# Two wide attention layers in one phase, with keys and values of the second layer's first two pairs projected before its normalised rows

## The chip, the cores and the metric

The kernel runs on one core of a Trainium2 chip. The metric is the device time of one execution in microseconds; less is better. The five engines are TensorE (PE in the rows; PEld is its weight load), VectorE (DVE), ScalarE (ACT), GpSimd (POOL) and SyncE (SP, which here only issues DMAs). Each runs its own program in order and waits for the others on semaphores.

## What is computed

A chain of four cross-attention modules on x, two batches of 256 rows and 256 features, against one context of 512 rows per batch. The first module has 16 narrow heads and an MLP. The second, in which the change lies, has two wide layers, 16 heads of 128 features each, and then an MLP. The third and fourth have 16 narrow heads each. One wide layer is, cut from the reference:

```python
def _cross_attention(q_in, kv_in, wq, bq, wk, bk, wv, bv, wo, bo, bias_k, bias_v):
    qh = (q_in @ wq + bq).reshape(b, q_len, H, K)
    kh = (kv_in @ wk + bk).reshape(b, t, H, K)
    vh = (kv_in @ wv + bv).reshape(b, t, H, K)
    kh = concatenate([kh, bias_k], axis=1); vh = concatenate([vh, bias_v], axis=1)
    weights = softmax(einsum('bqhk,bthk->bhqt', qh, kh) / sqrt(K))
    ctx = einsum('bhqt,bthk->bqhk', weights, vh).reshape(b, q_len, H * K)
    return ctx @ wo + bo

x = x + _cross_attention(_layer_norm(x, ln1_scale, ln1_offset), xf_1, ...)
x = x + _cross_attention(_layer_norm(x, ln2_scale, ln2_offset), xf_2, ...)
```

Both layers attend to the same context (xf_1 and xf_2 are the same tensor), with weights of their own. Only the queries depend on x. Everything is float32; products run as three matmuls on a high and a low part of each operand (`product3`, lines 82 to 84).

## The kernel before

`program` runs one `Phase` after another. A phase holds its buffers and semaphores, and at its end (line 140) it clears the semaphores and lets all engines meet at a barrier (its waits appear in rows as L141). `wide_attention` is one phase, run twice, for i = 1 and 2.

A wide layer works on 8 pairs of heads (`PAIRS`). For a pair there are ten projections of the pair's weights: two for queries, ("q", 0) and ("q", 1), four for keys and four for values (`PROJ`). Each is a job: PE fills one of four PSUM banks (`Ring`), ACT writes the high part from it to SBUF, and DVE writes the low part and frees the bank (lines 1189 or 1191, and 1238 or 1240). q, k, v, w, wo and stage are double-buffered by the pair's parity. The weights of pair p come by one DMA of SP into `stage`, and POOL scales and splits them: L1032, L1035 and L1036 for w, L1043 and L1044 for wo. For pair 0, ACT and DVE split the first three chunks (L1195, L1246), since POOL would be late.

A pair has four units (`UN`), one for each head and batch; g counts units. In the loop of unit g PE issues: scores of g, transposes of the probabilities of g - 1, projections for the next pair (`SHARES[u]`: 3, 3, 2 and 2), the output product of g - 2 into `sums`, and the product with V of g - 1. DVE takes the maximum (L1279), writes the low parts of the transposed probabilities, computes the inverse sums (L1290 to L1292), normalises the probabilities (L1294), and writes the low parts of projections and of the attended values. ACT takes the exponentials (L1215). The last pair of a layer has no next pair, so its units have no projections.

At the head of a layer, SP issues the first chunk of weights (the keys'), then four small loads (norm scales L703, `cols` L1012, `bk` L1013, `out_bias` L1014), then the other three chunks (L1008) and the weights of pair 1 (L1020). DVE computes row statistics of x (L111, L115, L123), POOL the root (`NormParts.root`, L711), DVE the normalised rows (L725), the two other weight splits, `bias_product` and the scaled `cols` (L1254, L1255), and adds the output bias to x, four operations (L1260). Only then it writes the low parts of the first four keys. PE projects four keys, then transposes the normalised rows (L740), which need the banks of the first keys, then four values, two queries and the small bias scores (L1129, L1131), and waits until DVE has their negative (L1270) before the first scores. POOL splits pair 1's weights right after pair 0's wo; for pair 2 it waits until the queries of pair 0 have been projected.

At the end of a layer, PE transposes the collected bias probabilities (L1160) after the last output product, ACT copies them (L1226), PE adds their product with the bias values (L1164), and DVE adds `sums` to x (L1304).

## Time and profile before

| | us |
|---|---|
| median of the timed runs | 1140.93 |
| lowest and highest of 3 | 1139.7, 1142.56 |
| span of the profiled execution | 1145.1 |
| its time with what lies around the span | not recorded; the span alone stands 4.2 above the median |
| first wide layer (head to the last bias product), in the profile | about 229 to 521 |
| second wide layer | about 521 to 815 |

The busy shares of the span are 84% for PE, 72% for DVE, 53% for ACT and 29% for POOL. They average stages with different limits: the two wide layers take half of the span, and what the change is worth must be read from the stretch around their border. A row of the timeline gives the start in us from the start of the span, the duration, engine, line, operation, what is written <- what is read with shapes, how many such instructions are merged, and in brackets how long the engine sat idle before and which engine ended that. Names carry no layer number: both layers' buffers are called L1a.

### The profile page before, as it was taken

What the parts mean: (1) busy time and instruction counts of PE and PEld (TensorE: products, weight loads), DVE (VectorE), ACT (ScalarE), POOL (GpSimd) and SP (SyncE); (2) the same over time, 40 slices, a digit from 0 to 9 for tenths busy, and PEclk for the clock granted to TensorE, in tenths of its full rate; (3) what the DMA queues carried; (4) which work ended last, traced back from release to release, by engine and by line L of the source; (5) the groups of instructions that cost most, each with busy time, mean ns of one, the idle gap of its engine ahead of it and who ended that gap; (6) DMA issues with size and microseconds to landing.
All of it is one profiled execution on the core that took longest, in us unless ns stands there. A gap on an engine that the chain in (4) does not pass through costs nothing. (4 is left out here: it accounts for less than half of the span.)

```text
span 1145.1 us, 17853 instructions
## 1 busy us (share of the span) xinstructions
PE 956.2 (84%) x6548; PEld 806.1 (70%) x6548; DVE 823.1 (72%) x1627; ACT 606.0 (53%) x1371; POOL 331.5 (29%) x324
## 2 busy tenths in 40 slices
PE   4788886569999999975999999998586798478958
PEld 3666665557888888963898899887475466465647
DVE  3377757976787887776678878777674587747865
ACT  2488873034555555642455556554424587257842
POOL 4245541441112222004102222200005355525520
PEclk8889998878999999997999999999798699789989
DMA  5985106140001110003101111000304920195120
GB/s 176 234 143 61 16 1 253 46 153 1 21 18 38 38 38 1 1 1 117 38 1 37 38 37 38 1 1 1 116 1 111 177 43 1 51 187 73 21 79 19
DMA packets 38242, 69.49 MB, mean 61 GB/s; under 512 B 7462, under 2 KB 23336, under 8 KB 35596
## 3 DMA queue, kind: packets, MB, share of 16 engines
q1 hardware_dynamic: 38156, 68.35, 24.6%
q8 instruction: 53, 0.87, 0.3%
q14 instruction: 33, 0.27, 0.1%
HBM read 57.31 MB, written 11.02 MB: 60 GB/s over the span
## 5 line engine op out<-in xcount | busy, mean ns | idle before, releaser
L1189 ACT CAST L1a_probsT_hi<-L1a_bank 128x512 fp32r<-128x512 f32 x128 | 68.8, 589 | 92.6 <-PE L1a_bank L1085 92.6
L1043 POOL TENSOR_SCALAR L1a_wo_hi<-L1a_stage 128x512 fp32r<-128x512 f32 x16 | 11.3, 707 | 347.8 <-PE L1a_sums L84 336.8
L1279 DVE TENSOR_REDUCE L1a_top<-L1a_scores 128x2 f32<-128x1024 f32 x64 | 78.2, 1222 | 35.2 <-PE L1a_scores L84 35.2
L1215 ACT ACTIVATE L1a_probs<-L1a_scores,L1a_neg_max 128x512 f32<-128x512 f32 x128 | 86.8, 684 | 30.3 <-DVE L1a_bias_shifted L1283 24.7
L82 PE MATMUL L1a_bank<-L1a_probsT_hi,L1a_v_hi 128*128 128x256 f32 x256 | 72.5, 283 | 11.7 <-DVE L1a_probsT_lo L1238 11.0
L1238 DVE TENSOR_TENSOR L1a_probsT_lo<-L1a_bank,L1a_probsT_hi 128x512 fp32r<-128x512 f32 x128 | 81.9, 681 | 0.1
L1191 ACT ACTIVATE L1a_attended_hi<-L1a_bank,L1a_cols 128x256 fp32r<-128x256 f32 x64 | 30.3, 474 | 91.5 <-PE L1a_bank L84 91.5
L82 PE MATMUL L1a_bank<-L1a_w_hi,ctxT_hi 128*128 128x256 f32 x256 | 75.7, 296 | 0.0
L83 PE MATMUL L1a_bank<-L1a_w_lo,ctxT_hi 128*128 128x256 f32 x256 | 73.1, 286 | 0.0
L84 PE MATMUL L1a_bank<-L1a_w_hi,ctxT_lo 128*128 128x256 f32 x256 | 73.0, 285 | 0.0
L400 POOL TENSOR_SCALAR L0a_probs<-L0a_probs,L0a_inverse 128x768 f32<-128x768 f32 x64 | 57.2, 906 | 53.2 <-DVE L0a_inverse L651 53.2
L637 DVE TENSOR_REDUCE L0a_neg_max<-L0a_scores 128x1 f32<-128x768 f32 x64 | 58.6, 954 | 18.1 <-PE L0a_scores L487 16.0
L84 PE MATMUL L1a_bank<-L1a_probsT_hi,L1a_v_lo 128*128 128x256 f32 x256 | 71.4, 279 | 0.0
L83 PE MATMUL L1a_bank<-L1a_probsT_lo,L1a_v_hi 128*128 128x256 f32 x256 | 71.4, 279 | 0.0
L1085 PE MATMUL L1a_bank<-ident,L1a_probs 128*128 128x128 f32 x512 | 66.2, 272 | 0.0
L82 PE MATMUL L1a_bank<-ctxT_hi,L1a_w_hi 128*128 128x512 f32 x128 | 53.5, 418 | 14.8 <-DVE L1a_w_lo L1246 14.8
L1085 PEld LDWEIGHTS L1a_bank<-ident,L1a_probs 128*128 128x128 f32 x512 | 59.6, 140 | 8.3
L576 ACT ACTIVATE L0a_probs<-L0a_scores,L0a_neg_max 128x768 f32<-128x768 f32 x64 | 57.5, 909 | 11.0 <-DVE L0a_neg_max L637 11.0
L82 PE MATMUL L1a_scores<-L1a_k_hi,L1a_q_hi 128*128 128x512 f32 x128 | 53.3, 416 | 10.8 <-DVE L1a_v_lo L1238 5.5
L1240 DVE SCALAR_TENSOR_TENSOR L1a_attended_lo<-L1a_bank,L1a_cols,L1a_attended_hi 128x256 fp32r<-128x256 f32 x64 | 30.9, 482 | 39.9 <-ACT L1a_attended_hi L1191 39.4
L82 PEld LDWEIGHTS L1a_bank<-L1a_probsT_hi,L1a_v_hi 128*128 128x128 f32 x256 | 48.2, 188 | 13.5 <-DVE L1a_probsT_lo L1238 12.4
L1294 DVE TENSOR_SCALAR L1a_probs<-L1a_probs,L1a_inverse 128x512 f32<-128x512 f32 x128 | 56.1, 480 | 0.0
(407 smaller groups left out, 3157.9 us busy)
## 6 DMA issues: line engine op xcount, KB each, us to landing
L1a_stage<-in_L_w SPq DMA_DIRECT2D x14, 1024.0 KB, 4.8
L0m_fold_wq<-in_L_wq SPq DMA_DIRECT2D x2, 2048.0 KB, 20.4
L0a_k_stack<-L0a_k_dram SPq DMA_DIRECT2D x12, 192.0 KB
L0a_w_qkv<-L0a_k_dram SPq DMA_DIRECT2D x12, 192.0 KB
L0a_probs<-in_L_wo SPq DMA_DIRECT2D x1, 2048.0 KB, 10.0
L0a_probsT<-in_L_wo SPq DMA_DIRECT2D x1, 2048.0 KB, 11.2
L0m_stage<-in_L_wm SPq DMA_DIRECT2D x4, 512.0 KB, 6.0
L0m_fold_bias_k<-in_L_bias_k SPq DMA_DIRECT2D x2, 1024.0 KB, 16.0
```

Source lines behind the costliest of these rows:

```text
L82: nc.tensor.matmul(out, lh, rh, start=start, stop=False, skip_group_check=loose)
L83: nc.tensor.matmul(out, lh, rl, start=False, stop=False, skip_group_check=loose)
L84: return nc.tensor.matmul(out, ll, rh, start=False, stop=stop, skip_group_check=loose)
L400: nc.gpsimd.tensor_scalar(probs[:, slot, :], probs[:, slot, :], inverse[:, small:small + 1], 1.0, ALU.mult, ALU.mult).then_inc(normed, 1)
L576: nc.scalar.activation(probs[:, m % probs_slots, :], slot_scores(m), ACT.Exp, bias=neg_max[:, small:small + 1], accum_out=row_sum[:, small ...
L637: nc.vector.tensor_reduce(neg_max[:, small:small + 1], slot_scores(m), AX.X, ALU.max, negate=True).then_inc(max_done, 1)
L1085: last = nc.tensor.transpose(ring.bank(job)[:, kt * P:(kt + 1) * P], probs[:, g % 2, qt, kt * P:(kt + 1) * P], keep["ident"][:, :])
L1189: nc.scalar.copy(out, source).then_inc(ring.hi_done, 1)
L1215: nc.scalar.activation(probs[:, g % 2, qt, :], scores[:, qt, :], ACT.Exp, bias=neg_max[:, g % 2, qt:qt + 1], accum_out=row_sum[:, g % 2, q ...
L1238: nc.vector.tensor_tensor(out[1], source, raw(out[0]), ALU.subtract).then_inc(ring.freed_by(job), 1)
L1279: link(nc.vector.tensor_reduce(top[:, :], scores[:, :, :], AX.X, ALU.max))
L1294: nc.vector.tensor_scalar(probs[:, s, qt, :], probs[:, s, qt, :], inverse[:, qt:qt + 1], None, ALU.mult).then_inc(normed, 1)
```

## The change

`wide_attentions` is one phase for both layers: `LAYERS` = 2, pairs 0 to 15 (`ALL`), units 0 to 63, one set of buffers. Small tensors exist once per layer (`cols`, `bk`, `out_bias`, `bias_product`, the norm's `scale_shift`); all of them are loaded at the head of layer 1, eight small loads instead of four, and both `bias_product` and `cols` are computed there. The buffers of the norm are shared.

- Units of pair 7 (the last of layer 1) project the keys and values of pair 8 (layer 2's first), two in each unit.
- After layer 1's last products PE projects the keys of pair 9, transposes layer 2's normalised rows, projects the values of pair 9, and then the queries of pair 8 and the bias scores (`queries`).
- Units of pair 8 project only the two queries of pair 9, in the first two units.
- POOL runs on through all 16 pairs; the root of layer 2's norm stands after the split of w and before the split of wo for pair 9.
- Between the layers DVE waits for `sums_full`, adds the sums to x and signals `sums_free`, for which the first output product of layer 2 waits.
- The transposes of the bias probabilities stand ahead of the last product with V, and ACT's copy ahead of its high part.

```diff
+    LAYERS = 2
+    ALL = LAYERS * PAIRS
     UN = 2 * B
+    GL = PAIRS * UN
     SK = S // P
     scale = float(DW) ** -0.5
-    PROJ = [("q", 0), ("q", 1), ("k", 0, 0), ("k", 0, 1), ("k", 1, 0), ("k", 1, 1)] + [("v", t) for t in range(0, CT, 2)]
-    SHARES = [PROJ[0:3], PROJ[3:6], PROJ[6:8], PROJ[8:10]]
-    FIRST = PROJ[2:]
+    QS = [("q", 0), ("q", 1)]
+    KV = [("k", 0, 0), ("k", 0, 1), ("k", 1, 0), ("k", 1, 1)] + [("v", t) for t in range(0, CT, 2)]
+    PROJ = QS + KV
+
+    def share(p, u):
+
+        if p == PAIRS:
+            return KV[2 * u:2 * u + 2]
+        if p == PAIRS + 1:
+            return QS[u:u + 1]
+        return (PROJ[0:3], PROJ[3:6], PROJ[6:8], PROJ[8:10])[u] if p < ALL else []
...
+        START = KV[:4] + ["norm0", "norm1"] + KV[4:] + QS + ["bias_scores"]
+        AGAIN = KV[:4] + ["norm0", "norm1"] + KV[4:] + QS + ["bias_scores"]
+        job_of, n = {}, 0
+        for item in START:
+            job_of[(0, item) if item in PROJ else (item, 0)] = n
+            n += 1
+        for layer in range(LAYERS):
+            if layer:
+                for item in AGAIN:
+
+                    job_of[(PAIRS + (item in KV), item) if item in PROJ else (item, layer)] = n
+                    n += 1
+            for gl in range(GL + 1):
+                g = layer * GL + gl
+                p, u = divmod(g, UN)
+                if gl:
+                    for qt in range(2):
+                        job_of["T", g - 1, qt] = n
+                        n += 1
+                if gl < GL:
+                    for item in share(p + 1, u):
+                        job_of[p + 1, item] = n
+                        n += 1
+                if gl == GL:
+                    job_of["bias", layer] = n
+                    n += 1
+                if gl:
+                    job_of["V", g - 1] = n
...
+                    for i in range(LAYERS):
+                        parts[i].load(sp, io)
+                        sp.dma_start(cols[i][:, :, :], io[f"L1_cols{i + 1}"]).then_inc(small_loaded, 16)
+                        sp.dma_start(bk[i][:, :], io[f"L1_bk{i + 1}"]).then_inc(small_loaded, 16)
+                        sp.dma_start(out_bias[i][:, :], io[f"L1_bo{i + 1}"].partition_broadcast(P)).then_inc(small_loaded, 16)
+            for p in range(1, ALL):
                 if p == 2:
                     sp.wait_ge(first_lo, 3)
                 if p >= 2:
                     sp.wait_ge(wo_ready, p - 1)
-                sp.dma_start(stage[p % 2][:, :], io[f"L1_w{i}"][p]).then_inc(loaded[p % 2], 16)
+                sp.dma_start(stage[p % 2][:, :], io[f"L1_w{p // PAIRS + 1}"][p % PAIRS]).then_inc(loaded[p % 2], 16)
...
+                if p == PAIRS + 1:
+                    parts[1].root(nc, pool)
                 if p >= 2:
                     pool.wait_ge(out_done, UN * (p - 1))
...
+                if g % GL == 0 and g:
+                    pe.wait_ge(sums_free, g // GL)
...
+            for layer in range(LAYERS):
+                if layer:
+                    pe.wait_ge(w_ready, PAIRS + 1)
+                for n, item in enumerate(KV):
+                    if n in (0, 4) and layer == 0:
+                        pe.wait_ge(first_lo, 1 if n == 0 else 2)
+                    project(PAIRS + 1 if layer else 0, item)
+                    if n == 3:
+                        parts[layer].transpose(nc, pe, ring, keep)
+                queries(layer)
+                for gl in range(GL + 1):
+                    g = layer * GL + gl
+                    p, u = divmod(g, UN)
+                    if gl < GL:
+                        if u == 0:
+                            for item in PROJ:
+                                ring.wait_evacuated(pe, job_of[p, item])
+                            if gl == 0:
+                                ring.wait_evacuated(pe, job_of["bias_scores", layer])
+                        score(g)
+                    if gl:
+                        transposes(g - 1)
+                    if gl < GL and p + 1 < ALL:
+                        if u == 0:
+                            pe.wait_ge(w_ready, p + 1)
+                        for item in share(p + 1, u):
+                            project(p + 1, item)
+                    if gl >= 2:
+                        output(g - 2)
+                    if gl == GL:
+                        bias_probabilities(layer)
+                    if gl:
+                        product_v(g - 1)
+                output(layer * GL + GL - 1)
+                bias_products(layer)
...
+                        job = job_of["bias", layer]
+                        act.wait_ge(ring.full, job + 1)
+                        nc.scalar.copy(bias_probsT[:, :], ring.bank(job)[:, :]).then_inc(ring.freed_by(job), 1)
+                    if gl:
+                        j, hh, b, h = unit(g - 1)
+                        high(job_of["V", g - 1], attended[(g - 1) % 2][0][:, :], cols[layer][:, 2, h:h + 1], Q)
...
+            for layer in range(LAYERS):
+                p0 = layer * PAIRS
+                if layer:
+                    dve.wait_ge(sums_full, layer)
+                    for t in range(RT):
+                        last = nc.vector.tensor_tensor(keep["x"][:, t, :], sums[:, t, :], keep["x"][:, t, :], ALU.add)
+                    last.then_inc(sums_free, 1)
+                    dve.wait_ge(sums_free, layer)
+                parts[layer].normalise(nc, dve, link, keep["x"], 1e-5, True)
+                if layer == 0:
+                    for n, c in enumerate(FIRST_ORDER[:3]):
+                        low_weights(n + 1, c)
+                    dve.wait_ge(small_loaded, 48 * LAYERS)
+                    for i in range(LAYERS):
+                        link(nc.vector.tensor_tensor(bias_product[i][:, :], cols[i][:, 0, :], cols[i][:, 1, :], ALU.mult))
+                        nc.vector.tensor_scalar(cols[i][:, 0, :], cols[i][:, 0, :], scale, None, ALU.mult).then_inc(cols_scaled, 1)
+                    dve.wait_ge(cols_scaled, LAYERS)
+                    dve.wait_ge(ones_set, 2)
+                dve.wait_ge(parts[layer].normed_ready, 1)
+                for t in range(RT):
+                    last = nc.vector.tensor_tensor(keep["x"][:, t, :], keep["x"][:, t, :], out_bias[layer][:, :], ALU.add)
+                last.then_inc(bias_ready, 1)
+                for n, item in enumerate(KV):
+                    p = p0 + 1 if layer else 0
+                    low(job_of[p, item], destination(p, item), bias_of(p, item))
+                    if n == 3:
+                        split_norm(layer)
```

## Rows read from the trace of the kernel before

**Rows 1.** Busy time by stretch: us, each engine's busy us (instructions), clock, DMA.
```profile
489.00:516.00 27.00, 20.71 (x150) 18.43 (x148) 19.32 (x46) 13.47 (x35) 0.00 (x0) 1.00 0.00 1
...
558.00:564.00 6.00, 5.73 (x18) 4.58 (x19) 1.76 (x4) 1.39 (x5) 0.16 (x1) 0.72 0.00 0
```

**Rows 2.** TensorE in order of time, at the border of the two wide layers.
```profile
519.12 1.99 PE L1164 MATMUL L1a_sums<-bias_values,L1a_bias_probsT 128*128 128x256 f32 x8 [0.68 <-ACT L1a_bias_probsT L1226]
528.76 0.79 PE L82 MATMUL L1a_bank<-ctxT_hi,L1a_w_hi 128*128 128x512 f32 x1 [7.66 <-DVE L1a_w_lo L1246]
...
542.10 1.94 PE L740 MATMUL L1a_bank<-ident,L1a_normed 128*128 128x128 f32 x8 [4.76 <-DVE L1a_k_lo L1240]
...
558.27 0.50 PE L82 MATMUL L1a_scores<-L1a_k_hi,L1a_q_hi 128*128 128x512 f32 x1 [2.65 <-DVE neg_bias_scores L1270]
```

**Rows 3.** VectorE in order of time, the same border.
```profile
521.15 1.42 DVE L1304 TENSOR_TENSOR x_rows<-L1a_sums,x_rows 128x256 f32<-128x256 f32 x4 [4.24 <-PE L1a_sums L1164]
523.49 1.41 DVE L111 BATCH_NORM_STATS2 L1a_stats<-x_rows 128x6 f32<-128x256 f32 x4 [0.93 <-PEq L141]
...
526.73 1.38 DVE L725 TENSOR_SCALAR L1a_normed<-x_rows,L1a_moments,L1a_rstd 128x256 f32<-128x256 f32 x4 [1.21 <-POOL L1a_rstd L711]
...
533.97 7.31 DVE L1260 TENSOR_TENSOR x_rows<-x_rows,L1a_out_bias 128x256 f32<-128x256 f32 x4
541.21 2.71 DVE L1240 SCALAR_TENSOR_TENSOR L1a_k_lo<-L1a_bank,L1a_bk,L1a_k_hi 128x512 fp32r<-128x512 f32 x4
```

**Rows 4.** GpSimd in order of time, the same border.
```profile
525.67 1.02 POOL L711 TENSOR_TENSOR L1a_rstd<-L1a_shifted,L1a_power 128x4 f32<-128x4 f32 x1 [1.50 <-DVE L1a_shifted L123]
...
537.54 3.47 POOL L1036 TENSOR_TENSOR L1a_w_lo<-L1a_stage,L1a_w_hi 128x1536 fp32r<-128x1536 f32 x1
540.98 0.79 POOL L1043 TENSOR_SCALAR L1a_wo_hi<-L1a_stage 128x512 fp32r<-128x512 f32 x1
...
543.20 0.62 POOL L1032 TENSOR_SCALAR L1a_stage<-L1a_stage 128x512 f32<-128x512 f32 x1
```

**Rows 5.** VectorE, normalised rows of the narrow layer L3a.
```profile
985.38 6.82 DVE L725 TENSOR_SCALAR L3a_normed<-x_rows,L3a_moments,L3a_rstd 128x256 f32<-128x256 f32 x4 [1.22 <-POOL L3a_rstd L711]
```

**Rows 6.** TensorE in order of time, units without projections and the layer's end.
```profile
499.70 0.39 PE L82 MATMUL L1a_scores<-L1a_k_hi,L1a_q_hi 128*128 128x512 f32 x1
...
504.20 0.36 PE L82 MATMUL L1a_bank<-L1a_probsT_hi,L1a_v_hi 128*128 128x256 f32 x1 [1.37 <-DVE L1a_probsT_lo L1238]
...
505.64 0.39 PE L82 MATMUL L1a_scores<-L1a_k_hi,L1a_q_hi 128*128 128x512 f32 x1
...
517.84 0.60 PE L1160 MATMUL L1a_bank<-ident,L1a_bias_probs 128*128 128x128 f32 x4
```

**Rows 7.** TensorE in order of time: starts of scores in units with projections.
```profile
455.86 0.50 PE L82 MATMUL L1a_scores<-L1a_k_hi,L1a_q_hi 128*128 128x512 f32 x1 [0.55 <-DVE L1a_v_lo L1238]
...
472.99 0.40 PE L82 MATMUL L1a_scores<-L1a_k_hi,L1a_q_hi 128*128 128x512 f32 x1
...
480.25 0.40 PE L82 MATMUL L1a_scores<-L1a_k_hi,L1a_q_hi 128*128 128x512 f32 x1
...
587.88 0.50 PE L82 MATMUL L1a_scores<-L1a_k_hi,L1a_q_hi 128*128 128x512 f32 x1
```

**Rows 8.** ScalarE in order of time, second exponential of layer 2's first unit.
```profile
563.29 0.68 ACT L1215 ACTIVATE L1a_probs<-L1a_scores,L1a_neg_max 128x512 f32<-128x512 f32 x1
```

**Rows 9.** VectorE in order of time, low parts of two queries.
```profile
565.46 1.40 DVE L1240 SCALAR_TENSOR_TENSOR L1a_q_lo<-L1a_bank,L1a_cols,L1a_q_hi 128x512 fp32r<-128x512 f32 x2
```

**Rows 10.** SyncE's issues in order of time, head of layer 1.
```profile
231.18 0.43 SPq L1014 DMA_DIRECT2D L1a_out_bias<-in_L_bo  x1
231.66 1.38 SPq L1008 DMA_DIRECT2D L1a_stage<-in_L_w  x3
```

**Rows 11.** ScalarE in order of time, head of layer 1: weight splits.
```profile
236.37 1.29 ACT L1195 ACTIVATE L1a_w_hi<-L1a_stage 128x512 fp32r<-128x512 f32 x2 [3.78 <-DMA L1a_stage<-in_L_w]
```

**Rows 12.** VectorE in order of time, head of layer 1: output bias onto x.
```profile
239.13 7.32 DVE L1260 TENSOR_TENSOR x_rows<-x_rows,L1a_out_bias 128x256 f32<-128x256 f32 x4
```

323 lines of the change are left out of this document (139 added, 184 removed).

## The prediction

> **What bounds the kernel now.** I read first the busy times by stretch, then TensorE (PE) in order of time across the border between the two wide layers, then VectorE (DVE), GpSimd (POOL) and ScalarE (ACT) over the same stretch, each time looking for what ended the last wait. Inside a wide layer PE is the bound: a unit of attention (one head, one batch) with two projections takes 7.26 us, 472.99 to 480.25, and PE has no gap in it [rows 7]. It stops being the bound where projections are missing. In a layer's last pair of heads there is nothing to project, and a unit takes 5.94 us [rows 6], with 1.37 us of idle PE in front of each product with V, ended by DVE's low part of the transposed probabilities. PE is busy 20.71 of 27 us there, at a granted clock of 1.00 [rows 1].
>
> The border is worse. PE ends the last bias product at 519.12 + 1.99 = 521.11. It starts the next keys at 528.76, because DVE has just split freshly loaded weights; it ends them at 542.10 - 4.76 = 537.34 and waits until 542.10 for a key's low part from DVE; it starts the first scores at 558.27 [rows 2]. From the last product to the transposes of the normalised rows pass 20.99 us. DVE's share of that: adding sums to x (from 521.15), 0.93 us of phase change, statistics, normalising (from 526.73), two weight splits, then four additions of the output bias that take 7.31 us together, and the keys' low parts from 541.21 [rows 3]. Those additions are long because POOL splits the weights of pair 1 beside them: its 3.47 us operation ends at 541.01, and the fourth addition ends at 541.28 [rows 3, 4]. Each of the four gets through in a gap between two POOL operations.
>
> **The change, part by part.** T is the end of layer 1's bias product, 521.11 before. I count pairs through both layers (0 to 7, 8 to 15) and units likewise (28 to 31 are pair 7, 32 to 35 pair 8).
>
> *The border (A).* One phase goes, with its barrier, its first weight load and the split of these weights on ACT and DVE: pair 9's keys and values are projected first, from weights that POOL split during pair 7. So PE starts keys at T and needs no more than the 8.6 us it took before at a mostly low clock, 528.76 to 537.34 [rows 2]. What is late next is DVE, in program order: sums into x until T + 1.46 (1.42 us, as at 521.15); statistics as before, which took from 523.49 to POOL's start at 525.67, 2.2 us, so POOL starts the root at T + 3.75 and ends it at T + 4.8 (1.02 us) [rows 3, 4]. Then come four normalising operations, 1.38 us undisturbed [rows 3]. They are not undisturbed now. POOL stands directly behind the root with wo of pair 9 and the scaling of pair 10's weights, three operations that took 540.98 to 543.82, 2.84 us [rows 4]. No row has this DVE line beside those POOL lines. Below: 1.38 us, ends at T + 6.2. Above: the same line in a later stage, beside POOL's memsets, took 6.82 us [rows 5], ends at T + 11.6. I take the middle way that the four bias additions show, one DVE operation for each gap of POOL: two or three wait, and the last ends some 0.35 us after POOL, at T + 8.1. The bias additions then find POOL waiting for the queries of pair 8, and cost about 1.4 us (as at 521.15, the same size) instead of 7.31: T + 9.5. The first low part of a key (4 in 2.71 us) frees the bank at T + 10.3, and the transposes start. PE's keys are done by T + 8.6 at the worst, so they stay hidden. Gain: 20.99 - 10.3 = 10.7 us. From the transposes to the first scores the order is unchanged, values, queries, bias scores, 16.17 us [rows 2]. The idle of PE ahead of the transposes stays about 4.7 us, so I keep the cold start of what follows.
>
> *Pair 7 gets eight projections (B).* Two in each unit, so its units become those of 7.26 us instead of 5.94 [rows 6, 7]: 4 x 1.32 = 5.3 us. POOL now also splits weights for pairs 8 and 9 during pairs 6 and 7, as in the middle of a layer. There it costs one DVE delay per pair, seen as 0.55 us of idle PE ahead of a unit's scores [rows 7]: 2 x 0.5. Cost 6.3 us. If more projections or waits hid in these units, the full pair's measured length already has them.
>
> *Pair 8 loses eight of ten (C).* Before: 558.27 to 587.88, 29.6 us [rows 2, 7]. After: unit 32 has one projection, and the next scores start when both exponentials are through: 563.29 + 0.68 = 563.97 [rows 8], so 5.8 us. Unit 33 is a thin unit of 5.94 with one query's low part, 1.40 / 2 = 0.7 us [rows 9], ahead of DVE's maximum: 6.6. Units 34 and 35 have none: 5.94 each. Sum 24.3, gain 5.3 us. So B and C are nearly a plain move: the hole in PE's work goes from pair 7 to pair 8.
>
> *Bias tail (D).* The transposes of the bias probabilities now stand before the product with V, which gives ACT time for the copy. Between 517.84 and 519.12 pass 1.28 us [rows 2, 6]; about 0.25 of it moves into the product's start, 1.0 us is saved, in both layers: 2.0 us.
>
> *Layer 1's head (E).* SP issues eight small loads instead of four between the first and second weight chunk. One costs 0.48 us of queue (231.18 to 231.66) [rows 10]: 1.9 us later for the values', queries' and wo chunks, and for the load of pair 1's weights behind them. Waiting on them are ACT, whose split of the second chunk started at 236.37 when its load landed [rows 11], and POOL; behind both stand DVE's bias additions (from 239.13) [rows 12] and the transposes. The small loads also take room on the DMA engines: 0 to 1 us more, I take 0.3. DVE has two more short operations ahead of the additions, which cost one gap of POOL, the 0.79 us operation of the kind at 540.98 [rows 4]: 0.7. Sum 2.9 us. Bounds: 0 (if the landing is hidden by other waits) and 5.7 (1.9, 1 us of traffic, and all three POOL operations of the 2.84 us above in the way).
>
> Sum: -10.7 + 6.3 - 5.3 - 2.0 + 2.9 = -8.8 us. The span of 1145.1 becomes 1136.3. The profiled execution is 4.2 us longer than the median of the timed runs; an absolute difference carries over, so the time is 1140.9 - 8.8 = 1132.1.
>
> **The rivals.**
> 1. *The border gives more.* The normalising operations pass before POOL starts (T + 6.2 instead of T + 8.1), the wait of PE shrinks to under 3 us, and the clock does not fall. For: DVE and POOL both start within 0.1 us of the root's end, 526.73 against 525.67 + 1.02 [rows 3, 4]. Against: 6.82 us in the other stage [rows 5]. Price 1.9 plus some 1.3 of warm transposes and values: 1128.9.
> 2. *The head costs its upper bound* and DVE and POOL meet once more in pairs 7 and 8 (1 us): 1132.1 + 2.8 + 1 = 1135.9. For: DMA rows say nothing of eight in a row.
> 3. *The clock stays low through pair 8 (slower).* The scores before unit 32 start after 2.65 us of waiting, and the clock granted from 558 to 564 is 0.72 of full speed, so part of it ran at 1.2 GHz and part at 2.4 [rows 1]. Before, ten projections in a dense row followed; now units with gaps. At 1.2 GHz the about 19 us of PE work of pair 8 (24.3 less four gaps of 0.9 to 1.4) take 38: + 14.3, so 1146.4. It decides from about 12 us of extra work time on, that is if nearly the whole pair runs low. Against it: units with the same gaps in pair 7 ran at 1.00 [rows 1, 6], though they entered warm. The Trainium skill (TensorE: Matmul & The Clock Gate, section on the second HAM failure mode, psum-queue depth-cycling) tells of a kernel whose short idle times between groups of matmuls made the clock swing between its levels; by it pair 8 would lie between 24.3 and 38 us, where my sum has 24.3, and the trace of thin units disagrees.
> 4. *The work ahead is not ahead.* If POOL split pair 9's weights only after T, PE would start its keys some 6 us late (0.62 of scaling, 3.47 for the low half and, I estimate, half of that for the high half [rows 4]), and the wait for DVE would hide all but about 2 to 4 us: 1135. Against: POOL is idle for most of a pair, and the stage buffer is free from pair 7's start.
>
> **How the numbers follow.** Forecast 0.58, with its own range 1129.5 to 1134.5; rival 1 0.18; rival 2 0.12; rival 4 0.04; rival 3 0.05; 0.03 for a slip of some microseconds that ends within no change. About 0.3%, or 3.4 us, is what a measurement of this kernel can tell from no change. Faster by more than that (under 1137.5): the first four and a part of their spread, 0.89; same 0.06; slower 0.05. The range 1126 to 1137 takes in the forecast and rivals 1, 2 and 4, with the spread of the timed runs (1139.7 to 1142.6) around them.
>
> **What would show it.** In the profile after: PE's keys follow the last bias product without a gap; transposes of normalised rows about 10.3 us after it; four normalising operations of 2.5 to 3.5 us together, beside POOL's wo, and four bias additions of about 1.4 us; pair 7 about 29.6 us and pair 8 about 24.3 us from scores to scores; a granted clock of 1.00 from some 8 us after the start of pair 8; bias products right behind the last output product; in layer 1's head the second chunk landing about 2 us later and the transposes about 3 us later. A clock of 0.5 in pair 8, bias additions still near 7 us in layer 2, or keys waiting for POOL's weights would make the prediction wrong.

## The result

| | us | ratio to the kernel before, 95% interval |
|---|---|---|
| before, 10 runs beside it | 1141.47 (1137.25 to 1147.08) | |
| changed kernel, 10 runs | 1135.98 (1129.81 to 1140.35) | 0.9945 [0.9921, 0.997] |
| changed kernel, once more, 7 runs | 1136.63 (1131.45 to 1141.13) | 0.993 [0.9905, 0.9956] |

The change makes the kernel faster, by 6.3 us in the first comparison (0.9945 of 1141.47; interval 3.4 to 9.0) and 8.0 us in the second (0.993 of 1144.24, the median of 24 runs of the kernel before beside it). The forecast was 8.8 us less, 1132.1, with 1126 to 1137 as range. The profiled span went from 1145.1 to 1131.1 us, 14 us less; that is more than the timed runs give, and the experiments will show why one pair of profiles can't be taken for the difference.

The page of the changed kernel, busy time of each engine and share of the span:

```profile
span 1131.1 us, 17854 instructions
PE 956.8 (85%) x6548; PEld 809.0 (72%) x6548; DVE 817.2 (72%) x1624; ACT 603.5 (53%) x1367; POOL 336.1 (30%) x325
```

Its busy times by stretch (duration, then busy us and instructions of PE, PEld, DVE, ACT, POOL, the granted clock, DMA share, GB/s); they answer [rows 1]. The first line is pair 7, which was thin (without projections) and is now filled; then come the stretch from the transposes of the normalised rows to layer 2's first scores, the first unit of pair 8, and the rest of pair 8:

```profile
493.00:522.00 29.00, 27.52 (x199) 25.50 (x198) 21.42 (x44) 14.99 (x35) 7.62 (x6) 1.00 0.10 37
533.00:550.00 17.00, 14.16 (x92) 13.60 (x93) 10.55 (x14) 5.51 (x9) 4.89 (x2) 0.80 0.05 19
550.00:557.00 7.00, 5.92 (x16) 4.40 (x17) 2.24 (x7) 2.12 (x6) 0.00 (x0) 0.68 0.00 0
557.00:576.00 19.00, 15.27 (x101) 13.25 (x100) 15.25 (x37) 9.85 (x25) 0.00 (x0) 1.00 0.01 1
```

PE has no hole left between the projections and products of pair 7 (27.5 of 29 us busy, where it was 20.7 of 27; the 1.5 us that are missing stand at its end, ahead of two output products). Pair 8 is the thin one now (15.3 of 19 us), and it runs at a granted clock of 1.00 from 557 on, though its first unit ran at a mean of 0.68.

TensorE of the changed kernel in order of time, at the border and through pair 8; it answers [rows 2, 6]:

```profile
521.04 1.89 PE L1149 MATMUL L1a_sums<-bias_values,L1a_bias_probsT 128*128 128x256 f32 x8
522.58 0.58 PE L72 MATMUL L1a_bank<-ctxT_hi,L1a_w_hi 128*128 128x512 f32 x1
...
533.00 1.94 PE L731 MATMUL L1a_bank<-ident,L1a_normed 128*128 128x128 f32 x8 [4.61 <-DVE L1a_k_lo L1287]
...
550.01 0.77 PE L72 MATMUL L1a_scores<-L1a_k_hi,L1a_q_hi 128*128 128x512 f32 x1 [2.85 <-DVE neg_bias_scores L1337]
...
556.17 0.50 PE L72 MATMUL L1a_scores<-L1a_k_hi,L1a_q_hi 128*128 128x512 f32 x1 [1.07 <-ACT L1a_probs L1262]
...
567.09 0.35 PE L72 MATMUL L1a_bank<-L1a_probsT_hi,L1a_v_hi 128*128 128x256 f32 x1 [1.37 <-DVE L1a_probsT_lo L1285]
...
574.60 0.40 PE L72 MATMUL L1a_scores<-L1a_k_hi,L1a_q_hi 128*128 128x512 f32 x1
```

The last bias product has no wait before it any more, and the keys of pair 9 start right behind it, with no idle time in brackets. The product ends at 521.04 + 1.89 = 522.93, the transposes of the normalised rows start at 533.00: 10.07 us, where it was 20.99. Pair 8 goes from 550.01 to 574.60, 24.6 us.

VectorE and then GpSimd over the same border, answering [rows 3] and [rows 4]:

```profile
522.97 1.42 DVE L1310 TENSOR_TENSOR x_rows<-L1a_sums,x_rows 128x256 f32<-128x256 f32 x4 [2.85 <-PE L1a_sums L1149]
524.42 1.41 DVE L101 BATCH_NORM_STATS2 L1a_stats<-x_rows 128x6 f32<-128x256 f32 x4
...
527.65 3.08 DVE L716 TENSOR_SCALAR L1a_normed<-x_rows,L1a_moments,L1a_rstd 128x256 f32<-128x256 f32 x4 [1.21 <-POOL L1a_rstd L702]
530.76 1.43 DVE L1325 TENSOR_TENSOR x_rows<-x_rows,L1a_out_bias 128x256 f32<-128x256 f32 x4
532.11 2.72 DVE L1287 SCALAR_TENSOR_TENSOR L1a_k_lo<-L1a_bank,L1a_bk,L1a_k_hi 128x512 fp32r<-128x512 f32 x4
```

```profile
506.83 0.11 POOL L699 MEMSET L1a_power<- 128x4 f32 x1
526.59 1.03 POOL L702 TENSOR_TENSOR L1a_rstd<-L1a_shifted,L1a_power 128x4 f32<-128x4 f32 x1 [19.64 <-DVE L1a_shifted L113]
527.60 0.62 POOL L1069 TENSOR_SCALAR L1a_wo_hi<-L1a_stage 128x512 fp32r<-128x512 f32 x1
528.30 1.26 POOL L1070 TENSOR_TENSOR L1a_wo_lo<-L1a_stage,L1a_wo_hi 128x512 fp32r<-128x512 f32 x1
529.65 0.62 POOL L1056 TENSOR_SCALAR L1a_stage<-L1a_stage 128x512 f32<-128x512 f32 x1
```

The phase change between sums and statistics is gone. POOL had w of pair 9 split by 506.83, 16 us ahead. The normalising operations take 3.08 us instead of 1.38, through POOL's three operations, and the four additions of the output bias take 1.43 us instead of 7.31.

All the profiles, cut at the same events, in us. "Head" is from the first weight load of layer 1 to its first scores; "border" from the end of layer 1's bias product to the transposes; "to scores" from there to layer 2's first scores; "pair 7" ends with the bias product; a steady pair is the median of pairs 1 to 5 and 9 to 13, scores to scores; "wide" is both layers together, from the first weight load to the first load of the MLP behind them. The kernels below changed are the experiments of the next section.

| kernel | head | border | to scores | pair 7 | pair 8 | steady pair | wide |
|---|---|---|---|---|---|---|---|
| before | 34.61 | 20.99 | 16.17 | 33.44 | 29.61 | 32.36 | 587.89 |
| before_again | 31.82 | 19.54 | 16.70 | 33.45 | 30.31 | 32.36 | 585.47 |
| changed | 32.83 | 10.07 | 17.01 | 37.14 | 24.59 | 32.51 | 576.16 |
| after_again | 36.70 | 10.07 | 17.11 | 37.17 | 24.61 | 32.51 | 580.05 |
| merged_only | 37.48 | 10.08 | 16.50 | 35.86 | 30.02 | 32.51 | 585.10 |
| spread | 32.95 | 10.07 | 14.16 | 37.13 | 25.60 | 32.52 | 574.21 |
| wo_later | 32.49 | 8.38 | 16.39 | 37.14 | 24.58 | 32.51 | 573.59 |
| neg_on_act | 30.44 | 10.08 | 14.77 | 37.15 | 24.62 | 32.52 | 569.77 |
| few_waits | 32.95 | 10.08 | 16.55 | 37.14 | 24.60 | 32.58 | 576.18 |
| wait_order | 36.04 | 10.07 | 17.56 | 37.17 | 24.57 | 32.33 | 577.49 |
| small_loads_later | 31.25 | 10.06 | 17.22 | 37.13 | 24.58 | 32.49 | 574.89 |
| head_pool_later | 29.14 | 10.06 | 17.00 | 37.14 | 24.57 | 32.52 | 572.02 |
| combined | 29.27 | 8.38 | 11.18 | 37.17 | 25.11 | 32.58 | 566.32 |
| combined_order | 29.11 | 8.36 | 11.60 | 37.17 | 25.63 | 32.33 | 563.87 |

Read the columns downwards. Border, pair 7, pair 8 and the steady pair are the same to a tenth or two wherever the code is the same. The head is not: it moves by 5 us between kernels with the same head.

### The profile page after: what moved, and what is told of

It reads as the page before. It is cut to its first block and busy times, and to the rows that moved or that the text cites. A ratio compares the mean times of both kernels' runs of the same rounds, so it can differ in the third digit from the quotient of the medians.

```text
span 1131.1 us, 17854 instructions
## 1 busy us (share of the span) xinstructions
PE 956.8 (85%) x6548; PEld 809.0 (72%) x6548; DVE 817.2 (72%) x1624; ACT 603.5 (53%) x1367; POOL 336.1 (30%) x325
## 5 line engine op out<-in xcount | busy, mean ns | idle before, releaser
L1069 POOL TENSOR_SCALAR L1a_wo_hi<-L1a_stage 128x512 fp32r<-128x512 f32 x16 | 10.3, 646 | 363.2 <-PE L1a_sums L74 355.6
L566 ACT ACTIVATE L0a_probs<-L0a_scores,L0a_neg_max 128x768 f32<-128x768 f32 x64 | 57.5, 909 | 10.6 <-DVE L0a_neg_max L627 10.6
L72 PEld LDWEIGHTS L1a_bank<-L1a_probsT_hi,L1a_v_hi 128*128 128x128 f32 x256 | 49.1, 192 | 10.9 <-DVE L1a_probsT_lo L1285 10.7
```

The lines of the kernel that those rows point to most:

```text
L72: nc.tensor.matmul(out, lh, rh, start=start, stop=False, skip_group_check=loose)
L566: nc.scalar.activation(probs[:, m % probs_slots, :], slot_scores(m), ACT.Exp, bias=neg_max[:, small:small + 1], accum_out=row_sum[:, small ...
```

## The experiments

Each experiment was timed beside runs of the kernel before of its own: 24 runs, median 1144.24 us, for before_again, after_again, merged_only and spread; 16 runs, 1145.15, for wo_later, neg_on_act, few_waits and combined; 11 runs, 1142.62, for wait_order, small_loads_later, head_pool_later and combined_order. So ratios are to be compared, not microseconds. The changed kernel's own is 0.993 [0.9905, 0.9956], and most experiments' intervals overlap it: by time alone only neg_on_act, combined and combined_order stand clear below it. What the others bring is read from the stretches of their profiles, one profile for each.

**The same two kernels again, and the merge without the work ahead.** The first two runs show how far the terms repeat. Expected of the kernel before:

> The kernel before, unchanged, for a second profile and for the spread between executions. Theory A (the change of time comes from the two wide layers, and the rest of the difference of the two profiled spans, 14.0 us, is chance): ratio to before 1.000; from the first issue of the wide phases to the first issue of the MLP behind them about 587.9 us again, the stretches ahead of it and behind it differing by 1 to 3 us from the first profile; steady pairs of heads again 32.35 us; the head of layer 1 (first issue to first scores) 34.6 us. Theory B (the head of layer 1 is itself chance, since it hangs on when a load lands): the head differs by more than 1 us from 34.6 us.

Of the changed kernel:

> The changed kernel, unchanged, for a second profile and a better ratio. Theory A (the sum of the prediction, corrected by the head of layer 1, that came out 1.8 us shorter instead of 2.9 us longer, and by 0.17 us for each pair of heads): 11 to 12 us less than before between the first issue of the wide phase and the MLP, ratio about 0.990. Theory B (the short head is chance and a second profile shows about 37 us there): ratio about 0.994, as in the ten runs at hand, and the head near 37 us in this profile.

before_again measured 1142.52 us, ratio 0.9994 [0.9972, 1.0015]; after_again 1136.63, 0.993. The wide part is 587.9 and 585.5 in the two profiles of before, 576.2 and 580.1 in the two of the change: 11.7 less by the first pair, 5.4 by the second, 8.6 on average. Of the 3.9 us between the two profiles of the changed kernel, the head has 3.87. In both runs it is theory B that came true: the head moves by 3 to 4 us from one execution to the next.

merged_only keeps the single phase and projects pair 8's keys and values at the border, as the kernel before did; pair 7 is thin again and pair 8 full.

```diff
         if p == PAIRS:
-            return KV[2 * u:2 * u + 2]
-        if p == PAIRS + 1:
-            return QS[u:u + 1]
+            return []
...
-                    pe.wait_ge(w_ready, PAIRS + 1)
+                    pe.wait_ge(w_ready, PAIRS)
...
-                    project(PAIRS + 1 if layer else 0, item)
+                    project(PAIRS if layer else 0, item)
```

> The merged phase without the work ahead: pair 7's units project nothing, the border projects the keys and values of pair 8 (pair 9 in the change), pair 8's units all ten of pair 9. Theory A (the projections ahead only move the hole in TensorE's work from pair 7 to pair 8): within 1.5 us of the changed kernel, rather 1 us faster; pair 7 about 24 us, pair 8 about 29.7 us. Theory B (the work ahead is what brings the gain, the merged phase alone little): 5 us or more slower than the changed kernel.

Measured: 1140.63 us, 0.9973 [0.9954, 0.9991], 3.1 us faster than before, and some 3 to 5 us slower than the change. That lies between the two theories, nearer to B. Its border is 10.08 us, as in the change: the whole gain of the border is the merge's, none is the moved projections'. What these bring lies in pairs 7 and 8: 35.86 + 30.02 = 65.9 us here, 37.14 + 24.59 = 61.7 in the change, 63.1 and 63.8 in the two profiles of before. The third of the four units of pair 7, VectorE, GpSimd and TensorE of merged_only (the product with V at 503.78 is the second unit's, undisturbed):

```profile
505.11 2.09 DVE L1360 TENSOR_SCALAR L1a_probs<-L1a_probs,L1a_inverse 128x512 f32<-128x512 f32 x2
...
508.76 1.76 DVE L1347 SCALAR_TENSOR_TENSOR L1a_neg_max<-L1a_top,neg_bias_scores 128x2 f32<-128x2 f32 x1
```

```profile
505.27 1.66 POOL L1057 TENSOR_SCALAR L1a_w_hi<-L1a_stage 128x1536 fp32r<-128x1536 f32 x1
507.00 3.49 POOL L1058 TENSOR_TENSOR L1a_w_lo<-L1a_stage,L1a_w_hi 128x1536 fp32r<-128x1536 f32 x1
```

```profile
503.78 0.35 PE L72 MATMUL L1a_bank<-L1a_probsT_hi,L1a_v_hi 128*128 128x256 f32 x1 [1.37 <-DVE L1a_probsT_lo L1283]
512.01 0.55 PE L72 MATMUL L1a_bank<-L1a_probsT_hi,L1a_v_hi 128*128 128x256 f32 x1 [3.33 <-DVE L1a_probsT_lo L1283]
```

DVE's operation on two columns (128x2, otherwise 0.16 us) takes 1.76 us, as it stands behind POOL's 3.49 us operation; the probabilities take 2.09 instead of 0.88. In a thin unit PE has nothing to do meanwhile: it is idle for 3.33 us instead of 1.37, and the unit takes 9.42 us. The two units before it, without the clash, take 6.1 and 6.0. In a filled unit two projections stand in between: in the change the same splits of POOL also run beside the third unit (one VectorE operation on two columns takes 1.82 us there), which takes 7.29 where its neighbours take 7.2. So a merge alone brings POOL's split for the next layer into a thin pair, and the projections ahead cover it there; pair 8, thin in their place, has no POOL work at all (POOL 0.00 in the windows above). It was not a plain move.

**The border's and the first scores' own waits.** wo_later puts POOL's wo of pair 9 behind DVE's additions:

```diff
                     parts[1].root(nc, pool)
+                    pool.wait_ge(bias_ready, 2)
```

> GpSimd starts the split of wo for pair 9 only when VectorE has added layer 2's output bias to x. Theory A (the normalising operations took 3.1 us instead of 1.4 because one of VectorE's operations passes in each gap between GpSimd's): they take 1.4 us, and from the end of layer 1's bias product to the transposes pass 8.4 instead of 10.1 us; 1.7 us less in all, perhaps 1 us more where TensorE's clock then has less idle time to fall in. Theory B (GpSimd's later start costs as much elsewhere, since wo of pair 9 or w of pair 10 come late): pairs 8 and 9 together become 1 us or more longer.

Measured: 1132.06 us, 0.9895 [0.9854, 0.9935]; border 8.38 us instead of 10.07, as theory A had it. VectorE of wo_later, the same line as at 527.65 above:

```profile
529.34 1.38 DVE L716 TENSOR_SCALAR L1a_normed<-x_rows,L1a_moments,L1a_rstd 128x256 f32<-128x256 f32 x4 [1.21 <-POOL L1a_rstd L702]
```

3.08 - 1.38 = 1.70 us, and the border is 1.69 us shorter. The meeting of the two engines, for which the prediction had no row, costs that much.

neg_on_act lets ACT write the negative bias scores straight from the bank, so that they don't go through DVE:

```diff
+                nc.scalar.mul(keep["neg_bias_scores"][:, :, :].rearrange("p t h -> p (t h)"), ring.bank(job)[:, 0:RT * H],
+                              -scale).then_inc(ring.freed_by(job), 1)
...
-                last = nc.vector.tensor_scalar(keep["neg_bias_scores"][:, :, :], keep["bias_scores"][:, :, :], -1.0, None, ALU.mult)
-                last.then_inc(ring.freed_by(job), 1)
```

> The negative of the bias scores comes from ScalarE, straight from the bank, instead of VectorE from SBUF. Theory A (VectorE's 64-column operation takes 2.3 us only because GpSimd's weight split runs beside it): the wait of TensorE ahead of the first scores of each layer falls from about 2.8 to 0.8 us, 2 us less for each layer, 4 us in all; from the transposes of the normalised rows to the first scores of layer 2 about 15.0 instead of 17.0 us. Theory B (the first operation of VectorE behind it, the maximum or the minimum, meets GpSimd in its place): the wait goes, but the first unit grows by the same.

Measured: 1129.68 us, 0.986 [0.9817, 0.9903]. The wait ahead of the first scores, TensorE of neg_on_act:

```profile
544.58 0.77 PE L72 MATMUL L1a_scores<-L1a_k_hi,L1a_q_hi 128*128 128x512 f32 x1 [0.62 <-ACT neg_bias_scores L1253]
```

0.62 us instead of 2.85. A multiplication of 64 columns had taken 2.30 us at the change, and 2.31 before, since it began inside POOL's 3.4 us split of w. Layer 1's first scores wait in the same way, 2.65 us before, and 0.52 here: a gain of over 2 us in each layer, as theory A had it. The wide part is 6.4 us shorter than in the profile of the changed kernel, though: 2.4 us in the head, 2.2 from layer 2's transposes to its scores, and 1.8 in the very first unit of layer 1. That last piece is clock. The unit, changed kernel and then neg_on_act:

```profile
260.50:267.90 7.40, 7.39 (x25) 5.95 (x26) 2.64 (x8) 2.70 (x7) 0.00 (x0) 0.74 0.01 2
```

```profile
259.14:264.70 5.56, 5.56 (x25) 4.58 (x25) 2.05 (x7) 2.15 (x7) 2.08 (x1) 1.00 0.01 3
```

It can't be booked to the edit: in combined the same scores also wait only 0.52 us, and the unit takes 7.13 us at a granted clock of 0.76.

spread leaves the last two values of pair 9 to pair 8's last two units:

```diff
-            return QS[u:u + 1]
+            return (QS[0:1], QS[1:2], KV[6:7], KV[7:8])[u]
...
-        AGAIN = KV[:4] + ["norm0", "norm1"] + KV[4:] + QS + ["bias_scores"]
+        AGAIN = KV[:4] + ["norm0", "norm1"] + KV[4:6] + QS + ["bias_scores"]
```

> Two of pair 9's four value projections move from the border into units 34 and 35, the two that have none. Theory A (a unit without projections has 1.4 us of idle TensorE, which just takes one projection of 1.44 us, while at the border each costs its full length): 2.5 to 3 us faster than the changed kernel, pair 8 still about 23.3 to 24 us, from the transposes of the normalised rows to the first scores 14.1 instead of 17.0 us. Theory B (the thin units are bound by VectorE, which also has to write the low parts of the moved values, 0.69 us each): pair 8 becomes 1.4 us or more longer and the gain shrinks to 1.5 us or less.

Measured: 1132.95 us, 0.989 [0.9862, 0.9918]. From the transposes to the scores 14.16 us instead of 17.01, and pair 8 25.60 instead of 24.59: 1.8 us net, between the two theories. What is projected at the border costs its full length. The value projected in pair 8's third unit costs nothing (6.01 us with and without it), the one in its fourth costs 1.0 us (7.02 instead of 6.02), and the next pair's scores then wait 0.85 us for its low part.

**The steady pairs.** The prediction has no term for pairs 1 to 6 and 9 to 14, whose code looks the same. They take 0.16 us more each. The waits at the head of a pair were written anew, though: ten instead of six. few_waits goes back to six, with the four values in the order of time:

```diff
-                            for item in PROJ:
+                            few = PROJ[-4:] + [("k", 1, 1), ("q", 1)]
+                            for item in (PROJ if p in (0, PAIRS, PAIRS + 1) else few):
```

> At the start of a pair TensorE waits for six projections' banks, as in the kernel before, instead of all ten; pairs 0, 8 and 9 keep the ten. Theory A (each wait that is already fulfilled still costs TensorE's sequencer some 40 ns, and the pair start is on TensorE's critical path): steady pairs 32.35 us again instead of 32.5, some 2 us less than the changed kernel over the two layers. Theory B (the 0.17 us per pair comes from somewhere else, such as the order of jobs in the banks): pairs stay at 32.5 us.

Measured: 1135.78 us, 0.9924 [0.9899, 0.9949]; the pairs take 32.58 us, not less but more. The theory that the pair's length goes with the number of fulfilled waits fell. wait_order has the same six in the order of the kernel before:

```diff
+                            late = [PROJ[-1], PROJ[-2], PROJ[-3], PROJ[-4], ("k", 1, 1), ("q", 1)]
```

> The changed kernel with the kernel before's waits at the start of a pair: six banks, the value projected last waited for first, the others after it. Nothing is left out of the computation. Question: where the 0.17 us per steady pair of eight units' work went (32.35 us before, 32.52 after, 32.57 with the six waits in the order of time). Theory 'order of the waits' (a fulfilled wait that stands between the late one and the scores costs nothing, one that stands after it in the queue does, or the reverse): the steady pairs go back to 32.35, so 13 pairs give 2.2 us, and the total is 2 us below the changed kernel's. Rival 'something else of the merge' (where the instructions or buffers lie, the products' pitch): the pairs stay at 32.5 and the total equals the changed kernel's within 1 us.

Measured: 1132.02 us, 0.9915 [0.9885, 0.9946]; the pairs take 32.33 us. That is the kernel before's length, from nothing but the order. The same place in the three kernels, end of a pair: DVE's last low part of the values and PE's next scores. The changed kernel:

```profile
354.11 1.28 DVE L1285 TENSOR_TENSOR L1a_v_lo<-L1a_bank,L1a_v_hi 128x512 fp32r<-128x512 f32 x2
```

```profile
355.65 0.47 PE L72 MATMUL L1a_scores<-L1a_k_hi,L1a_q_hi 128*128 128x512 f32 x1 [0.65 <-DVE L1a_v_lo L1285]
```

few_waits:

```profile
355.15 1.28 DVE L1286 TENSOR_TENSOR L1a_v_lo<-L1a_bank,L1a_v_hi 128x512 fp32r<-128x512 f32 x2
```

```profile
356.75 0.47 PE L72 MATMUL L1a_scores<-L1a_k_hi,L1a_q_hi 128*128 128x512 f32 x1 [0.72 <-issue]
```

wait_order:

```profile
358.92 1.28 DVE L1286 TENSOR_TENSOR L1a_v_lo<-L1a_bank,L1a_v_hi 128x512 fp32r<-128x512 f32 x2
```

```profile
360.25 0.50 PE L72 MATMUL L1a_scores<-L1a_k_hi,L1a_q_hi 128*128 128x512 f32 x1 [0.45 <-DVE L1a_v_lo L1286]
```

From the end of DVE's operation to the start of the scores: 355.65 - 355.39 = 0.26, 356.75 - 356.43 = 0.32, and 360.25 - 360.20 = 0.05 us. The traces show what lies between. Waits are instructions of PE's sequencer (EVENT_SEMAPHORE), each with up to two waits in it; L63 is the line of the bank waits, L1098 that of the wait for the exponentials, which shares its instruction with a bank wait. One more wait stands on the scores' first weight load itself. The views by line give the count in the window, the durations in ns and the first and last start. The changed kernel, from 355 us on: one instruction at 355.4, which passes once DVE's low part is written at 355.39, and one behind it.

```profile
L63 PEldq EVENT_SEMAPHORE  x1: 51/51/51, 355.4 to 355.4; - x1
L1098 PEldq EVENT_SEMAPHORE  x1: 51/51/51, 355.5 to 355.5; - x1
```

few_waits: the first instruction, begun at 353.7, blocks for 2.75 us until DVE is done, and two more follow it.

```profile
L63 PEldq EVENT_SEMAPHORE  x2: 51/1400/2749, 353.7 to 356.5; - x2
L1098 PEldq EVENT_SEMAPHORE  x1: 51/51/51, 356.6 to 356.6; - x1
```

wait_order: the last wait instruction has blocked for the exponentials and ended before DVE is done; the value's bank is waited for on the weight load.

```profile
L1098 PEldq EVENT_SEMAPHORE  x1: 1926/1926/1926, 357.7 to 357.7; - x1
```

| kernel | wait instructions ahead of the scores | the last value's bank is waited for in | from the low part to the scores |
|---|---|---|---|
| before, wait_order | 3 | the weight load | 0.05 |
| changed | 5 | the fourth | 0.25 |
| few_waits | 3 | the first | 0.32 |

So the gap goes with how many wait instructions stand behind the late one, and not with their total. The fulfilled ones follow each other at 0.105 us, and 0.08 us pass from the start of the last to that of the weight load: in the changed kernel 0.04 + 0.105 + 0.08 + 0.03 us to the first matmul. The order in the program is not that of the source: in wait_order the source names the last value's bank first, and its wait stands last of all.

**Layer 1's head.** small_loads_later issues the four small loads of layer 2 behind pair 1's weights, on a semaphore of their own, and prepares layer 2's `cols` on DVE after layer 1's queries:

```diff
-                    for i in range(LAYERS):
-                        parts[i].load(sp, io)
...
+                    small_loads(0, small_loaded)
             for p in range(1, ALL):
...
+                if p == 1:
+                    small_loads(1, small_loaded_again)
...
-                    dve.wait_ge(small_loaded, 48 * LAYERS)
-                    for i in range(LAYERS):
...
+                    dve.wait_ge(small_loaded, 48)
+                    prepare_cols(0)
```

> The changed kernel, but the four small loads of layer 2 are issued after pair 1's weights, and layer 2's columns are prepared on DVE after layer 1's queries. Nothing is left out. It undoes the part of the change that touches layer 1's head. My sum in the prediction: the second weight chunk is issued 1.9 us earlier and the transposes start 2.9 us earlier (head from the first issue to the first scores 29.5 to 34.5 us, total 1133). Rival 'chance': the head is set by whether DVE's four additions of the output bias meet POOL's three operations of wo and pair 1's scaling, and that varies from execution to execution by as much; then the head lies anywhere from 30 to 37 us as in the other runs, and the timed ratio moves by less than its interval, about 0.993 to 0.995.

head_pool_later leaves the loads as they are and lets POOL wait:

```diff
                     pool.wait_ge(loaded[j], 16 * (p // 2 + p % 2))
+                    if p == 1:
+                        ring.wait_evacuated(pool, job_of["norm1", 0])
```

> The changed kernel, but in layer 1's head POOL waits for the second bank of the normalised rows before it scales and splits pair 1's weights. Nothing is left out. If the head's length is the meeting of DVE's additions of the output bias with POOL's operations, these additions take 1.5 to 3.5 us instead of up to 6.6, the head lies near 30 us, and the total is 2 to 4 us below the changed kernel's (0.990 to 0.992). If the head's length is when the weight chunks land, it stays between 32 and 37 us and the total does not move.

Measured: small_loads_later 1129.27 us, 0.989 [0.9857, 0.9923], head 31.25 us; head_pool_later 1129.44 us, 0.9888 [0.9852, 0.9925], head 29.14 us. Three places, each VectorE's additions of the output bias and GpSimd's start of wo. The changed kernel (first load at 227.67):

```profile
238.40 2.94 DVE L1325 TENSOR_TENSOR x_rows<-x_rows,L1a_out_bias 128x256 f32<-128x256 f32 x4
```

```profile
238.52 0.79 POOL L1069 TENSOR_SCALAR L1a_wo_hi<-L1a_stage 128x512 fp32r<-128x512 f32 x1 [7.61 <-DMA L1a_stage<-in_L_w]
```

after_again, the same code (first load at 231.49):

```profile
244.28 6.62 DVE L1325 TENSOR_TENSOR x_rows<-x_rows,L1a_out_bias 128x256 f32<-128x256 f32 x4
```

```profile
241.49 1.14 POOL L1069 TENSOR_SCALAR L1a_wo_hi<-L1a_stage 128x512 fp32r<-128x512 f32 x1 [6.76 <-DMA L1a_stage<-in_L_w]
```

small_loads_later (first load at 227.75):

```profile
236.77 2.41 DVE L1335 TENSOR_TENSOR x_rows<-x_rows,L1a_out_bias 128x256 f32<-128x256 f32 x4
```

```profile
235.38 1.13 POOL L1074 TENSOR_SCALAR L1a_wo_hi<-L1a_stage 128x512 fp32r<-128x512 f32 x1 [4.39 <-DMA L1a_stage<-in_L_w]
```

Two things add up. One is systematic: POOL's wo, which starts when the last weight chunk lands, starts 7.6 to 8.3 us after the first load where there are four small loads ahead (before, before_again, small_loads_later), and 9.5 to 11.1 us after it in the other eleven profiles. The other is chance. The four additions of DVE take 2.4 to 3.4 us or 6.6 to 7.3 us and nothing between: either all four are through by the time POOL begins the longer split of pair 1's w (3.5 us), or one of them meets it and takes 3.6 us. Which case comes hangs on landings. With eight small loads and no later start of POOL, its wo begins 9.5 to 10.0 us after the first load in the three long cases and 10.6 to 11.1 in the five short ones: here an earlier landing goes with the longer head. Cut by these two cases, the heads without an edit of their own are:

| additions | four small loads ahead | eight small loads ahead |
|---|---|---|
| short | 31.82 (before_again), 31.25 (small_loads_later) | 32.83 (changed), 32.95 (spread), 32.95 (few_waits), 32.49 (wo_later) |
| long | 34.61 (before) | 36.70 (after_again), 37.48 (merged_only), 36.04 (wait_order) |

The four further small loads cost 1.3 us in the short case (31.5 to 32.8) and 2.1 in the long (34.6 to 36.7, one profile of before), and the case costs 3 to 4 us. In the short case DVE meets the same POOL operation later, in the first high part of the transposed rows (a cast of 3.32 us in the changed kernel, 0.42 otherwise), where about half of it is hidden: in the changed kernel the additions end 5.7 us sooner after the first load than in after_again, and the head is 3.9 us shorter. In head_pool_later the additions can't meet the splits of pair 1's w, and take 1.43 us (2.94 in combined, which has the same edit: POOL's wo can still stand beside them). Its head is the shortest of those with eight small loads and no other edit, 3.7 us below the short case, and 2.1 us of that are the wait ahead of the first scores, 0.63 us instead of 2.7, since here their negative falls into the gap between two splits of POOL (0.19 us); that, too, is a matter of when things meet. So both theories named for small_loads_later hold a part: the loads cost their 1.3 to 2.1 us, and a single profile can't show it, since the case moves more.

**All together.** combined has spread, neg_on_act, wo_later, head_pool_later and few_waits in one kernel; combined_order has wait_order in place of few_waits.

> Spread, few waits, the negative on ScalarE, wo later, and in layer 1's head GpSimd starts the split of pair 1's weights only when the normalised rows are split. By the single parts: spread 1.9 us, waits 2 us, negative 4 us, wo 1.7 us, together 9 to 10 us less than the changed kernel; the head of layer 1, which took 31.8 to 37.5 us in six profiles, should come out at its short end each time, near 30 us, since VectorE meets GpSimd nowhere in it: another 2 to 5 us. Sum 11 to 14 us less than the changed kernel, a ratio to before near 0.982. Theory B (the parts share one chain, TensorE's own work becomes the bound): less than 8 us.

> The combined kernel (last value projected in the last unit, ScalarE writes the negative bias scores, POOL's wo of pair 9 after the bias additions, POOL later in layer 1's head) with the six waits of a pair's start in the order of the kernel before. Nothing is left out. If the order of the waits is worth the 0.2 us per steady pair, it is 2 to 3 us below combined, some 1121 to 1122 us (0.979); if not, it equals it at 1124 (0.981).

Measured: combined 1124.1 us, 0.9811 [0.9776, 0.9847]; combined_order 1122.07 us, 0.9825 [0.9792, 0.9858]. Each was timed beside its own runs of before (medians 1145.15 and 1142.62), and by their ratios the two can't be told apart. Their profiles can: the wide part is 566.3 and 563.9 us, and the steady pairs 32.58 and 32.33. Both beat both kernels, the kernel before by 20 to 22 us. In its profile combined is 10 to 14 us below the two of the changed kernel, near the 11 to 14 that the single parts gave. The first unit of layer 2, from these scores on, still takes 6.18 us at a granted clock of 0.52 in combined_order; in combined it takes 4.9 at 1.00. TensorE of combined_order, the first scores of layer 2 and of the second unit:

```profile
538.97 0.77 PE L72 MATMUL L1a_scores<-L1a_k_hi,L1a_q_hi 128*128 128x512 f32 x1 [0.63 <-ACT neg_bias_scores L1257]
...
545.15 0.51 PE L72 MATMUL L1a_scores<-L1a_k_hi,L1a_q_hi 128*128 128x512 f32 x1 [0.73 <-ACT L1a_probs L1268]
```

## Why the prediction was right, and where not

| term | forecast | measured, mean of two profiles each |
|---|---|---|
| A, border | -10.7 | -10.2 (20.27 to 10.07) |
| B, pair 7 filled, clashes in pairs 6 and 7 | +6.3 | +5.5 (+3.7 in pair 7 with its tail, 1.3 of the tail added back, +0.5 in pair 6) |
| C, pair 8 | -5.3 | -5.4 (29.96 to 24.60) |
| D, bias tail, both layers | -2.0 | -2.6 (33.56 to 32.28 in pair 15, pair 7 taken as the same) |
| E, head of layer 1 | +2.9 | +1.6 (33.22 to 34.77), within one case +1.3 or +2.1 |
| steady pairs | 0 | +1.8 (0.8 in pairs 0 to 6 without B's share, 1.0 in pairs 9 to 14) |
| from the transposes to the scores | 0 | +0.6 (16.44 to 17.06) |
| wide layers | -8.8 | -8.6 (586.7 to 578.1) |

The terms of the right column sum to -8.6 before rounding, and the timed runs gave -6.3 and -8.0 with intervals of some 3 us to either side. The size of the large terms and their mechanism were right; the timed gain is 0.8 to 2.5 us short of the forecast, less than those intervals. That the sum agrees to 0.2 us is partly luck: B, D and E were forecast 2.7 us too dear together, and that paid for 2.4 us which had no term and for A.

**A.** The steps came out in the forecast's order. From T = 522.93: POOL starts the root at T + 3.66 (forecast 3.75), the normalising ends at T + 7.8 (8.1), the bias additions at T + 9.3 (9.5), the transposes start at T + 10.07 (10.3). The middle way between the two far bounds of the normalising, 1.38 and 6.82 us [rows 3, 5], was the right choice: 3.08. It was argued from how the bias additions get through between POOL's operations [rows 3, 4], and wo_later shows that POOL's operations are the whole cause of the difference. The Trainium skill (SBUF — State Buffer, "Who interferes with whom") says that a VectorE instruction with two inputs in SBUF contends with a GpSimd instruction that reads SBUF, that one in a mode with two ports contends with GpSimd too, and that whoever issues first holds the shared pair of ports for the whole instruction. The trace agrees: the additions of the output bias, with both inputs in SBUF, go from 1.43 to 7.31 us, and the writing of low parts from banks keeps its 2.7 us for four [rows 3].

**B and C.** Both sizes were right, and the sentence "nearly a plain move" was wrong. It compares the thin pair 7 of before with the thin pair 8 of the change, but the kernel without the move is merged_only, whose pair 7 has POOL's splits in it. Against that the move brings 4.2 us: a thin unit suffers from the clash in full (9.42 us instead of 6.0) and a filled one hides it (7.29 instead of 7.2). The sum was right because pair 8 was priced without POOL work, from rows that had none either.

**D.** Right, 0.3 us more than forecast in layer 2's tail; layer 1's, now part of a filled pair, is taken as the same and was not measured by itself.

**E.** The term was mis-sized and, in one pair of profiles, had the wrong sign: the head went from 34.61 to 32.83. The step that failed was to take one profile of before as the base. Its additions of 7.32 us [rows 12] were a long case; before_again's took 2.4. The 1.9 us of queue that SP's four issues cost [rows 10] lies between what the two cases show (1.3 and 2.1); the 1.0 us put on top of it was too much. Of that, the 0.3 us for traffic of the small loads had no row, and no run shows it by itself.

**What had no term.** The steady pairs, whose code I took as unchanged, cost 1.8 us through the order of their waits. The 0.55 us of idle PE ahead of a pair's scores [rows 7] was read as a delay of DVE, and it is that; the row of the change says 0.65, with the same releaser, and only beside DVE's end can it be seen that the delay is PE's own. The 0.6 us between the transposes and the scores is clock. The stretch has the same matmuls in all these profiles, and what differs is PE's busy time in it. Before, changed and wait_order:

```profile
542.10:558.27 16.17, 13.52 (x92) 12.93 (x93) 10.55 (x14) 5.50 (x9) 6.52 (x4) 0.91 0.20 67
```

```profile
533.00:550.01 17.01, 14.16 (x92) 13.61 (x93) 10.55 (x14) 5.51 (x9) 4.89 (x2) 0.80 0.05 19
```

```profile
536.84:554.40 17.56, 14.71 (x93) 14.16 (x93) 10.54 (x14) 5.50 (x9) 4.89 (x2) 0.79 0.04 16
```

The rest of the stretch is 2.65 to 2.85 us each time. The prediction said that the cold start stays as it was; in two profiles of before the mean granted clock is 0.91 and 0.84, in the changed kernel's two 0.80. Why the clock rises later in some executions of equal code (16.55 to 17.56 us) stays open.

**Rivals.** Rival 1 (the border gives more) had its condition only where wo was moved, in wo_later and the two combined kernels: in wo_later the border is 8.4 us and the wait shrinks to 2.9, but the clock falls all the same (0.81 in the stretch behind it, against 0.80), and of the 1.3 us for warm transposes and values at most 0.6 came (16.39 us instead of 17.01). Rival 2 (head at its upper bound) looks like after_again and merged_only, with heads of 36.7 and 37.5 us, but their length is the long case, which the kernel before has as well. Rival 3 (the clock stays low in pair 8) fell (its price, too, was added wrongly: 38 less 24.3 are 13.7, not 14.3): the granted clock is 0.68 of full speed in the first 7 us, where it went from 1.2 to 2.4 GHz, and 1.00 in the 19 us after them, with holes of 1.0 to 1.4 us before each product with V. By the rule that the prediction cites there from the Trainium skill (TensorE: Matmul & The Clock Gate, the second HAM failure mode), pair 8 would have been longer; 24.6 us and the 1.00 behind the first unit show none of it. Rival 4 (the weights come late) fell: POOL was done at 506.83.

## What to carry to other kernels

Price a merge of two stages with two numbers: the chain that is late next at the seam (here statistics, root, normalising, in DVE's program order), and what the producer of the next stage's data, now running earlier, collides with while its neighbours are thin. Fill thin stretches with work that has no late input, and keep the other engine's long operations out of them. When waits are rewritten, compare the gap between the releasing operation's end and the waiting one's start in both traces, and find among the wait instructions the one that ends last: no other should stand behind it. And take the base of a term from two profiles at least where a load's landing decides who meets whom.

## What the hardware showed beyond that

On TensorE a fulfilled wait is not free when it stands behind one that blocks. With the late wait on the weight load itself the matmul starts 0.05 us after the release; with one wait instruction behind the late one it is 0.25 us, with two 0.32, and the instructions follow each other at 0.105 us. Standing ahead of the late wait they cost nothing. That came to 1.8 us here. And a VectorE operation of 0.16 us on two columns can cost 1.76 us behind a GpSimd operation of 3.49 us, and one on 64 columns 2.30 us behind one of 3.42; the price is set by how much of the other engine's operation is left, not by its own size.
